# Causal self-attention loop of a two-layer cross-attention kernel: chunk 0's probabilities through the transposing DMA, attended later

## The reference, cut to what matters

```python
# layer 0: masked cross-attention with projection, then an MLP; then layer 1, of which this is the part that matters
def _mha(x, kv, Wq, Wk, Wv, mask, causal):          # here kv is x and causal is True
    Q = einsum('bsd,hdk->bhsk', x, Wq) * m;  K = ... ;  V = ...
    energy = einsum('bhsk,bhtk->bhst', Q, K)
    lengths = sum(energy[:, :, 0, :] != 0, axis=-1)
    energy = where(cols >= lengths[:, :, None, None], -inf, energy)
    energy = where(cols[None, :] > cols[:, None], -inf, energy)      # causal
    score = softmax(energy / sqrt(dk), axis=-1)
    return einsum('bhst,bhtk->bhsk', score, V) * m
x1 = _layernorm(x + z, ln1_g, ln1_b)                # z is the result above
# then a second attention over the context, a feed-forward pair and two more layer norms
```

## Time and profile before

| what | value |
|---|---|
| median of 3 runs | 2639.27 us (2639.25 to 2640.81) |
| profiled execution, its own time | 2641.75 us |
| span of the profiled execution | 2640.0 us |
| TensorE busy over the span | 2585.4 us (98%) |
| VectorE, ScalarE, GpSimd busy over the span | 1940.1 us (73%), 1553.5 us (59%), 923.6 us (35%) |
| granted TensorE clock, mean | 0.994 of full speed |

### The profile page before, as it was taken

One profiled execution on the slowest core, in us unless ns is written; L12 is line 12 of the kernel. 1 busy time (PEld: TensorE's weight loads), 2 busy tenths in 40 slices (PEclk: granted clock), 3 DMA queues, 4 the chain that ended last, 5 costly groups with the idle time before them and its releaser, 6 DMA issues.

```text
span 2640.0 us, 67260 instructions
## 1 busy us (share of the span) xinstructions
PE 2585.4 (98%) x23144; PEld 2230.3 (84%) x23144; DVE 1940.1 (73%) x5443; ACT 1553.5 (59%) x4738; POOL 923.6 (35%) x1102
## 2 busy tenths in 40 slices
PE   6999999999999999999999999999999999999997
PEld 5888888887888888888888888888788888888886
DVE  7888898887433444345388888888788888888877
ACT  6778778785111111111287777777676776767764
POOL 5776677751101010101013333333333434334341
PEclk8999999999999999999999999999999999999999
DMA  6676677674211111203021111112322212222210
GB/s 190 162 189 172 174 171 179 174 181 136 64 48 55 41 51 44 63 32 106 21 82 48 48 48 48 48 48 81 117 73 71 88 64 74 85 65 98 68 48 25
DMA packets 313622, 236.12 MB, mean 89 GB/s; under 512 B 150736, under 2 KB 240848, under 8 KB 312656
## 3 DMA queue, kind: packets, MB, share of 16 engines
q1 hardware_dynamic: 313552, 235.22, 31.3%
HBM read 137.65 MB, written 63.96 MB: 76 GB/s over the span
## 4 chain that ended last, share of the span: by engine, by line
PE 75%; DVE 11%; ACT 8%; issue 5%; DMA 1%; POOL 0%; DVEq 0%; SPq 0%; ACTq 0%; POOLq 0%
PE cross_work L181 16%; PE mlp_f L3282 13%; PE mlp_acc L3300 13%; PE causal_work L181 10%; PE cross_scores L2298 3%; PE cross_scores L2275 2%; PE cross_attended L2328 2%; PE causal_scores L2298 2%; ACT mask_prob L975 2%; PE causal_scores L2275 2%; DVE mask_scores L1560 2%; PE mask_work L181 2%; ACT mask_prob_even L975 2%; PE causal_attended L2328 2%; DVE mask_stats L1473 1%
## 5 line engine op out<-in xcount | busy, mean ns | idle before, releaser
L3075 ACT ACTIVATE mlp_h<-mlp_f,mlp_b1col 128x512 f32<-128x512 f32 x128 | 88.3, 690 | 526.6 <-PE mlp_f L3282 526.6
L3282 PE MATMUL mlp_f<-mlp_xT_hi,mlp_w 128*128 128x512 f32 x1024 | 335.4, 389 | 0.0
L3182 DVE CAST mlp_hT_hi<-mlp_h 128x512 fp32r<-128x512 f32 x128 | 58.3, 455 | 369.8 <-ACT mlp_h L3075 369.6
L3300 PE MATMUL mlp_acc<-mlp_w,mlp_hT_hi 128*128 128x512 f32 x1024 | 315.2, 389 | 0.0
L975 ACT ACTIVATE cross_prob<-cross_scores,cross_low 128x256 f32<-128x256 f32 x512 | 237.5, 490 | 63.4 <-DVE cross_low L1554 63.4
L975 ACT ACTIVATE causal_prob<-causal_scores,causal_low 128x128 f32<-128x128 f32 (+1 forms) x512 | 210.6, 437 | 93.7 <-DVE causal_low L1560 93.6
L3282 PEld LDWEIGHTS mlp_f<-mlp_xT_hi,mlp_w 128*128 128x128 f32 x1024 | 192.1, 188 | 40.6 <-DVE mlp_xT_lo L3168 0.4
L3300 PEld LDWEIGHTS mlp_acc<-mlp_w,mlp_hT_hi 128*128 128x128 f32 x1024 | 192.2, 188 | 39.9
L1560 DVE CUSTOM_DVE_ANT_0 mask_scores<-mask_scores,mask_mask 128x256 f32<-128x256 f32 x512 | 200.5, 459 | 28.7 <-PE mask_scores L2275 24.2
L181 PE MATMUL causal_work<-causal_xT_hi,causal_w 128*128 128x256 f32 x1008 | 217.0, 293 | 0.3 <-DVE causal_qk_parts L1508 0.3
L736 POOL TENSOR_SCALAR causal_q<-all_own_head,causal_qk_parts 128x128 fp32r<-128x128 f32 x128 | 60.7, 486 | 405.9 <-DVE causal_qk_parts L1508 395.6
(11 more groups left out here) (370 smaller groups left out, 8072.4 us busy)
## 6 DMA issues: line engine op xcount, KB each, us to landing
cross_x_in<-after_attention SPq DMA_DIRECT2D x17, 512.0 KB, 4.0
mask_x_in<-in_x SPq DMA_DIRECT2D x16, 512.0 KB, 4.5
mask_c_in<-in_ctx SPq DMA_DIRECT2D x16, 512.0 KB, 4.8
mask_res<-in_x SPq DMA_DIRECT2D x16, 512.0 KB, 3.7
after_attention<-mask_res SPq DMA_DIRECT2D x16, 512.0 KB, 3.3
mlp_x<-after_attention SPq DMA_DIRECT2D x8, 1024.0 KB, 5.5
mlp_stage<-in_L_xattn_fc_w SPq DMA_DIRECT2D x8, 1024.0 KB, 5.7
after_layer<-mlp_y SPq DMA_DIRECT2D x8, 1024.0 KB, 4.4
```

What stands on the lines that cost most here:

```text
L3282: ins = pe.matmul(F1[m % 2][:], W[2 * (m // 4)][:, a, k, m % 4 * P:(m % 4 + 1) * P], xT[p][:, k, :], start=(k == 0 and n == 0), stop=(k == ...
L3300: ins = pe.matmul(ACC[t][:], hT[a][:, m % 2, t * P:(t + 1) * P], W[2 * (m // 4) + 1][:, p, m % 4, :], start=(m == 0 and n == 0), stop=(m = ...
```

## The change

In the 14 turns of the hardware loop (turns 1 to 14) chunk 0 is treated as the even chunks of the mask phase are. Its exponentials go to a tile of their own (`prob_even`), with a bias that lifts them by a constant (`lift` on VectorE, four small sums in a turn). ScalarE makes the high halves (`causal_high`), GpSimd the low halves (`causal_low`), and SyncE issues two transposing transfers (`causal_over`), ahead of the loads of rows. The values of those four heads are split in three bf16 parts (`values_high` and `values_middle` on ScalarE, `values_left` and `values_low` on GpSimd), and `causal_parts` attends with fp16 pairs. The four `turn_probs` and four `copy` of chunk 0 are gone.

The order is written anew for each engine in the loop. On TensorE the pair of chunks 0 and 1 is attended behind the scores of chunk 3 and the queries that follow them, the row-0 energies of chunk 3 follow the scores of chunk 2 at once, and halves of products that stood apart now stand together. On VectorE `add_z` stands after chunk 2's minima, and `row_stats` and `ln_var` after chunk 3's minima instead of before them. GpSimd keeps its order of the older steps, with the new ones between. Turns 0 and 15 keep the old form.

```diff
+        def causal_over(b):
+
+            hold(sp, s["av_done"], KC * b - KC + 1, s)
+            for i in range(2):
+                hold(sp, s["p_low"], 4 * b + 2 * i + 2, s)
+                sp.dma_start_transpose(PT16[:, i].rearrange("p a u k s -> p (a u k) s"),
+                                       P16[:, i].rearrange("p a u n -> p (a u n)")).then_inc(s["probs_turned"], IT)
...
+            over = causal and (not isinstance(b, int) or b == B - 2)
+            if over:
+                causal_over(b)
...
+        def causal_low(b, i):
+
+            pool.wait_ge(s["p_high"], 2 * b - 2 + i + 1)
+            for u in range(2):
+                pool.tensor_tensor(P16[:, i, 1, u], prob_even[i][:, u], P16[:, i, 0, u], ALU.subtract
+                                   ).then_inc(s["p_low"], 1)
...
+            if causal and not isinstance(b, int):
+                query0(b, 1)
+                causal_low(b, 0)
+                query0(b, 2)
+                causal_low(b, 1)
+                query0(b, 3)
+                values_left(b)
+                values_low(b)
+                query0(b + 1, 0)
+                last_norm(b)
+                last_gain(b)
+                return
...
+            if causal and crossed(b, c):
+                act.wait_ge(s["lifted"], HC * b - HC + h + 1)
+                if h == 0:
+                    act.wait_ge(s["p_low"], 4 * b)
...
-                act.wait_ge(s["av_done"], KC * b + c - 1)
+                act.wait_ge(s["av_done"], KC * b + ((2 if c == 3 else 0) if causal and not isinstance(b, int) else c - 1))
...
+        def causal_high(b, i):
+
+            if i == 0:
+                act.wait_ge(s["probs_turned"], IT * 2 * b)
+            act.wait_ge(s["exp_done"], UNITS * b + 2 * i + 2)
+            act.activation(P16[:, i, 0], prob_even[i][:], ACT.Copy).then_inc(s["p_high"], 1)
...
+        def causal_loop(b):
+
+            minima(b, 0)
+            cuts(b, 1)
+            attended(b, -2, 2)
+            qk_lo(b, 2)
+            turn_over(b + 1, 0)
+
+            minima(b, 1)
+            turn_over(b + 1, 1)
+            cuts(b, 2)
+            values(b, 1)
+            qk_lo(b, 3)
+            turned(b + 1, 0)
+            turned(b + 1, 1)
+
+            minima(b, 2)
+            cuts(b, 3)
+            add_z(b)
+            rows_kept(b)
+            qk_lo(b + 1, 0)
+
+            minima(b, 3)
+            row_stats()
+            ln_var(b, 0)
+            rows_seen(b + 1)
+            attended(b, 0, 2)
+            cuts(b + 1, 0)
+            qk_lo(b + 1, 1)
...
+        def causal_parts(b, c):
+
+            pe.wait_ge(s["probs_turned"], IT * (2 * b + 2))
+            pe.wait_ge(s["v_low"], b)
+            at = S * c
+            for kt in range(TT):
+                for n, (a, v) in enumerate(PARTS16):
+                    for h in range(HC):
+                        ins = pe.matmul(O[h * DH:(h + 1) * DH, at + kt * P:at + S],
+                                        VP[v][:, kt, h * DH:(h + 1) * DH],
+                                        PT16[:, h // 2, a, h % 2, 2 * kt:2 + kt, :],
+                                        start=(kt == 0 and n == 0), stop=(kt == 1 and n == len(PARTS16) - 1))
+            ins.then_inc(s["av_done"], 1)
...
+        def causal_loop(b):
+
+            turn_probs(b, -1)
+            scores(b, 0)
+            attend(b, -2, 2)
+            pe.wait_ge(s["qk_lo"], KC * b + 2)
+            queries(b, 2)
+            attended(b, -2, 2)
+            energies0(b, 1)
+            keys(b, 2)
+            pe.wait_ge(s["v_ready"], 2 * b + 1)
+            values(b, 1, 0)
+
+            scores(b, 1)
+            pe.wait_ge(s["qk_lo"], KC * b + 3)
+            queries(b, 3)
+            keys(b, 3, 0)
+            energies0(b, 2)
+            turn_probs(b, 4)
+            keys(b, 3, 1)
+            turn_probs(b, 5)
+            turn_probs(b, 6)
+            values(b, 1, 1)
+            turn_probs(b, 7)
+
+            scores(b, 2)
+            energies0(b, 3)
+            pe.wait_ge(s["t_lo"], NP * (b + 1) + 1)
+            pe.wait_ge(s["qk_lo"], KC * (b + 1))
+            queries(b + 1, 0, 0)
+            pe.wait_ge(s["t_lo"], NP * (b + 2))
+            queries(b + 1, 0, 1)
+            keys(b + 1, 0)
+            turn_probs(b, 8)
+            turn_probs(b, 9)
+            values(b + 1, 0, 0)
+            turn_probs(b, 10)
+            turn_probs(b, 11)
+
+            scores(b, 3)
+            pe.wait_ge(s["qk_lo"], KC * (b + 1) + 1)
+            queries(b + 1, 1)
+            attend(b, 0, 2)
+            keys(b + 1, 1)
+            attended(b, 0, 2)
+            energies0(b + 1, 0)
+            turn_probs(b, 12)
+            turn_probs(b, 13)
+            turn_probs(b, 14)
+            values(b + 1, 0, 1)
```

More of the change, by code:

```diff
@@ L171, in turned_by_pe @@
 def turned_by_pe(kind):
-    return KC // 2 * HC if kind == "mask" else UNITS
+    return {"mask": UNITS // 2 * B, "causal": 2 * UNITS + (UNITS - HC) * (B - 2), "cross": UNITS * B}[kind]
 def product(pe, out, lhs, rhs, half=None):
@@ L266, in attention_phase @@
         xT = [rest(f"xT_{part}", [P, KC, S], F32R) for part in ("hi", "lo")]
-        probT = rest("probT", [P, 8, 512])
+        probT = rest("probT", [P, 8, 512] if cross else [P, 8, 3 * P])
+        if causal:
+            rest("spare", [P, 8 * P])
         prob = rest("prob", [P, 4, TT, S])
@@ L277, in attention_phase @@
         sums = r("sums", [P, KC // 2, TT, 2 * HC])
-        low = r("low", [P, 4, TT])
+        if cross:
+            low = r("low", [P, 4, TT])
+        else:
+            lifted = r("lifted", [P, 4, TT])
         rs = r("rs", [P, TT, 2 * HC])
@@ L609, in sync @@
         if causal:
+            sp.sem_inc(s["probs_turned"], 2 * IT)
             yield ROOM
         yield from turn(0, prev=False, late=False)
-        yield from turn(1, late=False)
-        with sp.Fori(2, B - 2) as b:
-            yield from turn(b)
+        if causal:
+            with sp.Fori(1, B - 2) as b:
+                yield from turn(b)
+        else:
+            yield from turn(1, late=False)
+            with sp.Fori(2, B - 2) as b:
+                yield from turn(b)
         yield from turn(B - 2, after=False)
@@ L1328, in turn @@
                 cross_turn(b, prev, cur, nxt) if cur else cross_end(b)
+            elif causal and not isinstance(b, int):
+                causal_loop(b)
             else:
```

102 lines of the change are left out of this document (82 added, 20 removed).

## The result

| what | before | after |
|---|---|---|
| median | 2639.3 us (2639.25 to 2640.81) | 2694.4 us (2687.6 to 2695.88) |
| ratio | | 1.0202, 95% interval 1.0185 to 1.022 |
| span of the profiled execution | 2640.0 us | 2694.1 us |
| one looped turn at full clock | 32.70 us | 35.36 us |
| looped turns that lose time to half clock | 0 of 14 | 9 of 14 |

Forecast were 2675.5 us and a range of 2650 to 2688. The sign and the two long waits came as forecast; 19 us of the loss did not. Three of the four executions took 2694.2 us or more and one took 2687.6; the profile is of the slowest, 2695.88.

The account below looks back on a forecast made before the run. TensorE's own work was taken to set the turn. Segments gave +2.6 us per turn (terms: -1.0 + 1.9 + 1.7 + 0.4 = 3.0), 36 us over 14 turns, so 2675.5 us from the median 2639.27; range 2650 to 2688.

Parts of the forecast that it names:

- the sum: Adding up one looped turn on TensorE: 35.3 us against 32.7, times 14 turns 36 us slower; chance 0.64.
- The walk: Following TensorE's looped turn segment by segment, with the engines feeding it, to a period of 35.3 us.
- Wait one: TensorE, behind chunk 2's scores, waits for GpSimd's query before chunk 3's row-0 energies: 1.9 us in each turn.
- The rival of the short query: GpSimd's query for chunk 3 slips in ahead of VectorE's subtractions, taking 0.72 us, giving 2662; chance 0.08.
- Wait two: TensorE waits before chunk 1's row-0 energies for GpSimd's query, delayed by the later norm: 1.7 us, turns 2 to 15.
- The copy's wait: Ahead of chunk 3's scores TensorE waits for unit 10's copy: 0.4 us, bounds 0 and 0.8.
- The saved work: TensorE's work per turn falls by 1.0 us, bounds 0.6 to 1.6.
- four turns back: Turning chunk 0's four units of probabilities on TensorE, work that goes away: 1.3 us, between 1.0 and 1.7.
- by the segments: Turn added up between starts of scores and energies on TensorE: +2.6 us per turn, the figure taken.
- by the terms: Saved work and three waits added: -1.0 + 1.9 + 1.7 + 0.4 = 3.0 us per turn.
- a third wait of VectorE or GpSimd: VectorE's chain at the turn's end or GpSimd's low halves add 1 us or more: 2690 to 2700; chance 0.08.
- With no waits at all 2625: Limit of the not-slower rival, chunk 3's query in time: only saved work counts, -14 us; rival's chance 0.07.

Follow-up runs that it names:

- e1: Kernel after, with TensorE's row-0 energies of chunk 3 behind the next batch's queries and keys instead of straight behind chunk 2's scores; 2664.4 us.
- e4: Kernel after, with 20 unused identity transposes on TensorE between chunk 2's scores and chunk 3's row-0 energies; 2684.3 us.
- e5: Kernel before, with TensorE's row-0 energies of chunk 3 directly behind chunk 2's scores in the looped turns; 2680.5 us.
- e6: Kernel after, with VectorE's low parts of chunk 3's query ahead of its copy of chunk 1's values; 2669.1 us.
- e9: e8 with ScalarE copying chunk 3's queries and keys ahead of units 5 and 6, and VectorE adding z in two halves; 2646.2 us.
- e14: e9 with chunk 3's energies behind the queries' first half, ScalarE's turned rows ahead of unit 7's copy, its middle values copy behind unit 10's; 2637.8 us.
- e13: e14 with the second half of VectorE's adds of z behind chunk 3's cut instead of ahead of the low parts; 2654.6 us.
- e2: Kernel after, with VectorE's row statistics and ln_var ahead of chunk 3's minima again; 2663.1 us.
- e7: e6 with VectorE's sum z and row statistics up to ln_var moved ahead, behind the cuts of chunks 2 and 3; 2660.8 us.
- e8: e7 with TensorE's turn of unit 10 ahead of the first half of the next batch's values; 2659.1 us.
- e3: Kernel after, with the edits of both e1 and e2; 2667.1 us.

## Why the prediction was wrong

**The step that failed** is that the sum took every microsecond of TensorE at full speed. "At a clock of 1.00" was read from the earlier trace rows, and no term asked whether that holds once there are idle gaps. The missing term is 9 x 1.49 = 13.4 us in the loop and 1.6 us in turn 15 (S0 to S1 12.82, against 11.24 in e1, where turn 15 has the same wait of 1.86 and no fall), together 15.0. e4 (the gap filled) and e5 (the gap alone, in the kernel before) show it from both sides. With it the forecast would have been 2690.5; measured were 2694.4.

**The walk was right to 0.1 us in its sum.** A turn at full clock takes 35.36 us, forecast 35.3. Segment by segment: S3 to the energies of chunk 1 15.22 for 15.4; from there to S1 3.38 for 3.3; S1 to S2 7.23 for 7.2; S2 to S3 9.53 for 9.4. In its terms that is in part luck, as the next paragraphs show.

**Wait one** is 1.89 us, forecast 1.9, and the query takes 1.67, forecast 1.68. The rival of the short query had no part in it. By the Trainium skill's rule (SBUF — State Buffer, Who interferes with whom), that a VectorE instruction with two SBUF inputs shuts GpSimd's reads out, e6 and e9 should differ as they do. The traces agree: 0.72 us with 0.80 us of lead in e9, and in e6, with 0.33, a query of 1.78 beside subtractions of 1.29, or one of 1.22 beside subtractions of 1.43, so that sometimes the one and sometimes the other gives way. That this lock makes the query long was tried by the start alone, not by other operands.

**Wait two** is 1.06 us, forecast 1.7. GpSimd was 0.2 us earlier (query ready at S3 + 15.17 for 15.35), and TensorE 0.5 us later (S3 + 14.16 for 13.7). **The copy's wait** is 0.25, forecast 0.4.

**The saved work** was 0.54 us, under the lower bound of 0.6, forecast 1.0. S0 to S1 lost 9.10 - (9.13 - 1.06) = 1.03 us, where four turns back were priced at 1.3. S2 to S3 lost 9.12 - (9.53 - 1.89 - 0.25) = 1.73, and S3 to S0 gained 9.47 - 7.25 = 2.22, so the two segments together cost 0.49 more than before, where 0.3 was forecast. Only 0.14 of this is the attended pair itself (0.83 + 0.75 = 1.58 for 1.44, with the fp16 parts at their lower bound). From start to start the turns of the probabilities take 0.25 more and the two row-0 energies 0.17 more, with other instructions next to them; the forecast had no such term. The error in the work and that of the waits (3.20 for 4.0) pull in opposite directions: 2.66 measured, 2.6 by the segments, 3.0 by the terms. The prediction put wait two on turns 2 to 15, so a wait in turn 15 was in it; this one came out at 1.86 us and not 1.06.

**Range and rivals.** With the waits as forecast and nothing else, 2675.5 would stand; the upper end was set by a third wait of VectorE or GpSimd, and the clock was not among the rivals. "With no waits at all 2625" was reached by no run. The nearest is e14, which has 0.5 us of waits left in a turn of 32.5 us; with 32.0 us of busy time in a turn, 14 turns without waits would save some 10 us (an estimate), so about 2630. e13 shows that VectorE has no room to take the last waits away in that way.

**What stays open.** Why the same wait brings a fall in one turn and not in the next is not settled: waits of 1.89 us gave nine half-clock turns in the kernel after and one in e2, waits of 1.65 gave two in e7 and five in e8. The length of the gap alone does not decide it. Nor is it shown whether wait two, after which the clock never fell in the loop, has a share in the nine: without it, in e2, there was one. Each of these counts is of a single execution.

## What to carry to other kernels

A wait put into an engine that was never idle costs more than its length, if that engine's clock follows its activity: here 14 waits of 1.9 us cost 27 us, and up to 13 more. Before a call is moved forward in an engine's order, walk the other engines' chain that feeds it; the work that is moved out was its cover. And when two waits are to be removed, look which engine was using each of them as slack: here each repair alone gave some 30 us and both together no more than either.

## What the runs showed of the hardware

- TensorE's granted clock fell from 1.00 to 0.50 at the end of an idle gap of 1.5 to 1.9 us or up to 1.6 us behind it (0.5 to 1.6 us behind it in the kernel after), in some turns and not in others, and stayed there some 3.4 us (1446.8 to 1450.3 in the turn shown). It never fell in the loop in the runs e1, e3, e4 and e9 to e14, whose gaps there were 1.1 us or less. The Trainium skill (TensorE: Matmul & The Clock Gate, What's actually happening) says that the clock is set by how busy TensorE has been; the traces agree, and e4 shows that useless products count as work.
- The same GpSimd query, started 0.33 us ahead of the same VectorE subtractions, took 1.75 to 1.78 us in six turns of e6 and 1.22 us in eight; in those eight the subtractions took 1.43 us for 1.29.
- A VectorE cut (line 1638), 0.35 us as a rule, took 1.43 us in e3 beside GpSimd's last steps of the norm, and 0.55 in the kernel after.
